# First self attention of a Perceiver block: order of the weight loads, of the masked keys and bias adds, and of the first tile's scores

## The chip, the cores and the metric

The kernel runs on one core of a Trainium2 chip. The metric is the device time in microseconds of one execution, the median of several.

## The reference

The kernel computes one forward pass over x (16 sequences of 64 rows, 256 wide; 1024 rows in all) and a context of 1601 rows for each sequence, in float32. Six layers follow each other, each added to x and each behind a layer norm: cross attention to the context, the self attention with rotary positions that the change touches, a mixture of eight experts, a mean of the context, a second self attention, and a grouped feed forward. The one that matters here:

```python
x = x + _L0_attn_ref(_layernorm(x, axis=-1), L0_attn_w_qkv, L0_attn_w_out, L0_attn_b_out)

def _L0_attn_ref(x, w_qkv, w_out, b_out):      # H = 16 heads of 16
    q, k, v = jnp.split(x @ w_qkv, 3, axis=-1)
    q, k, v = (heads(q), heads(k), heads(v))
    q = q * cos + rotate_half(q) * sin
    k = k * cos + rotate_half(k) * sin
    dots = jnp.einsum('bhid,bhjd->bhij', q, k) * hd ** (-0.5)
    attn = jax.nn.softmax(dots, axis=-1)
    out = jnp.einsum('bhij,bhjd->bhid', attn, v)
    return out.transpose(0, 2, 1, 3).reshape(b, n, H * hd) @ w_out + b_out
```

## The kernel before

The program is one chain of blocks; in a block each engine has its own hand-written order of instructions, tied together by semaphores, and all engines meet at the end of a block. The 1024 rows are T = 8 tiles of 128 rows (two sequences each). The queries and keys of the first six tiles of this attention are projected early, inside the cross attention, and stored in DRAM (early_out, L297); the last two tiles (columns 768 to 1023) and the values of all eight are projected in `self_attention`.

The block ahead of it is `layer_norm` (L735 to L769). Its SP queue issues the loads that it is given: the six weights q, qr, k, kr, v and o (qr and kr are the weights with turned columns, for the rotary term) and the bias row, all seven counted on one semaphore, w_in. PE turns the normalised rows, ACT and DVE copy them to lnT.

In `self_attention` with rope and early (the first use, tag "sa"):

- SP (L910 to L915) waits for the early queries and keys to be in DRAM, loads them to QT and KTt counted on early_in, and then issues the loads of the experts' weights, some 12 MB.
- PE waits for w_in in full (L926), then computes the values in 8 units of 16 matmuls, n = 0 to 7, into two banks in turn (L928). DVE takes the even units out of the banks (L1059), ACT the odd ones (L1179). Both write to Vd, which DVE and POOL have set to zeros and ones before (L893, L894). Then come 8 projection units of 6 matmuls, in the order q, qr for two chunks and k, kr for two chunks (L942), in the same two banks: unit m waits for the taking out of unit m - 2. DVE multiplies a unit with the cosines (L1078), or with the sines (L1082) and adds (L1084). The weights are used as a high part made by ACT (L1187) and a low part made by POOL (L1025).
- After all projections (`projected(pe, 2)`) PE computes the scores of tile 0 (L958), and then runs over the tiles: in step t the scores of tile t + 1, the turning of the output of t - 1 (L986), the transposes of the probabilities (L967), the output projection of t - 1 (L994), the weighing of the values (L977). There is one pair of banks for the scores, SC, so scores t + 1 wait for DVE's subtraction of tile t.
- The scores need masked keys, Km: for each of four head rows a copy of the keys with the other rows zeroed. ACT makes the first (L1141), POOL the other three in two chunks (L1035, six operations for a tile). There are two buffers of them; tiles 0 and 1 are made ahead, tile t + 2 after the scores of tile t.
- POOL: zeros and ones, four weight splits, then the bias adds to X (eight operations, L788, in `add_bias`), then Km of tiles 0 and 1, then `projected(pool, 2)` and the others.
- DVE: after the last projection, per tile the maximum over each head's scores (L1099) and its subtraction (L1101), `less_max`; the normalising (L1108, L1110); and the adding of the output to X (L1116) with its statistics (L1119).
- ACT: values placed to Vt (L1135), keys (L1141), `projected(act, 2)`, then per tile the exponentials (L1148), the copy of the transposes (L1154) and of the turned output (L1160).

The second self attention (tag "sb") calls the same function without early and rope, and its keys need no mask.

## Time and profile before

| | us |
|---|---|
| median of 3 runs | 1307.55 |
| lowest and highest | 1303.25, 1313.32 |
| the profiled execution's time | 1307.01 |
| its span, first to last instruction | 1305.2 |
| PE busy | 1169.1 |
| DVE busy | 690.0 |
| ACT busy | 576.6 |
| POOL busy | 413.7 |

Times in the profile are microseconds from the start of the span unless ns is written. PE is TensorE's matmuls, PEld its weight loads, DVE VectorE, ACT ScalarE, POOL GpSimd, SP the engine that issues the transfers. A row of the timeline gives start, duration, engine, line, operation, output and inputs, shape and count, and in brackets the idle time before it and what ended it. The granted clock (PEclk) is TensorE's: 1.00 is 2.4 GHz, 0.50 is 1.2 GHz.

### The profile page before, as it was taken

To read this page: it belongs to the slowest core of one execution; us is meant where nothing else is said; L and a number is where in the kernel's file an instruction comes from. 1 tells how busy PE (TensorE), PEld (TensorE's weight loads), DVE (VectorE), ACT (ScalarE), POOL (GpSimd) and SP (SyncE) were. 2 spreads that over 40 slices of the span, in tenths; PEclk is the share of its full clock that TensorE was granted. 3 is DMA by queue.
4 is the path that set the end of the run, shared out by engine and by line. 5 is a ranking of instruction groups with operands and counts; after the bars stand their busy time and mean duration, and the time that the engine had idled before them with its cause. 6 is when DMAs were issued, how large, how long until landed. Compare 5 with 4: busy or idle time off the path is not lost. (4 is left out here: it accounts for less than half of the span.)

```text
span 1305.2 us, 32520 instructions
## 1 busy us (share of the span) xinstructions
PE 1169.1 (90%) x13911; PEld 1030.4 (79%) x13911; DVE 690.0 (53%) x1100; ACT 576.6 (44%) x953; POOL 413.7 (32%) x369
## 2 busy tenths in 40 slices
PE   4799999999999999999999999768796999288799
PEld 4789989999999999989999888656674777266588
DVE  6555655655655655655654743347462221564732
ACT  4465555555555555555555565326421232121400
POOL 5632432432432432432432416453351000522000
PEclk9899999999999999999999999979797999588999
DMA  6937646746746746746656743192021111405055
GB/s 200 212 79 170 159 92 159 164 97 163 159 98 161 163 97 157 163 100 160 157 104 147 165 89 78 51 365 107 10 97 52 53 61 53 133 10 213 2 186 190
DMA packets 63143, 165.70 MB, mean 127 GB/s; under 512 B 25032, under 2 KB 38424, under 8 KB 59928
## 3 DMA queue, kind: packets, MB, share of 16 engines
q1 hardware_dynamic: 60312, 158.37, 47.7%
q0 software_dynamic: 1536, 4.20, 0.9%
q8 instruction: 111, 1.82, 0.6%
q10 hardware_dynamic: 1152, 1.05, 0.2%
q14 instruction: 32, 0.26, 0.1%
HBM read 73.18 MB, written 11.01 MB: 65 GB/s over the span
## 5 line engine op out<-in xcount | busy, mean ns | idle before, releaser
L504 DVE TENSOR_REDUCE xa_mx<-xa_sc 128x2 f32<-128x804 f32 x256 | 243.3, 991 | 42.1 <-PE xa_sc L665 42.1
L458 ACT ACTIVATE xa_pt<-xa_sc 128x1024 f32<-128x1024 f32 (+1 forms) x224 | 212.3, 963 | 108.7 <-PE xa_sc L681 108.4
L681 PE MATMUL xa_sc<-xa_queries,xa_keys 104*128 104x128 f32 (+1 forms) x1664 | 221.5, 276 | 0.9 <-issue 0.4
L681 PEld LDWEIGHTS xa_sc<-xa_queries,xa_keys 104*128 104x128 f32 (+1 forms) x1664 | 196.5, 187 | 18.1 <-issue 4.5
L590 PE MATMUL xa_pj<-xa_ctx_hi,xa_wk 128*128 128x400 f32 (+1 forms) x512 | 157.6, 350 | 1.2 <-DVE xa_qst L532 0.9
L590 PE MATMUL xa_pj<-xa_wv,xa_ctx_hi 128*128 128x256 f32 (+1 forms) x832 | 155.2, 285 | 0.1
L692 PE MATMUL xa_op<-xa_pt,xa_values 128*32 128x64 f32 x6656 | 136.3, 222 | 9.0 <-ACT xa_pt L458 4.1
L665 PE MATMUL xa_sc<-xa_keys,xa_queries 96*128 96x402 f32 x512 | 134.5, 364 | 10.8 <-DMA xa_keys<-xa_kst_hi 7.5
L337 POOL TENSOR_TENSOR xa_ctx_lo<-xa_raw,xa_ctx_hi 128x1600 fp32r<-128x1600 f32 (+1 forms) x32 | 115.9, 3624 | 78.0 <-DVE xa_ctx_hi L497 75.3
L342 POOL TENSOR_TENSOR xa_kst_lo<-xa_wk,xa_kst_hi 128x400 fp32r<-128x400 f32 x64 | 67.4, 1053 | 228.4 <-ACT xa_kst_hi L411 228.3
L590 PEld LDWEIGHTS xa_pj<-xa_wv,xa_ctx_hi 128*128 128x128 f32 (+1 forms) x832 | 126.1, 184 | 7.9 <-issue 6.3
L692 PEld LDWEIGHTS xa_op<-xa_pt,xa_values 128*32 128x32 f32 x6656 | 103.5, 109 | 28.0 <-ACT xa_pt L458 15.8
L590 PE MATMUL xa_pj<-xa_wv,xa_ctx_lo 128*128 128x256 f32 (+1 forms) x416 | 116.4, 280 | 0.0
L424 ACT ACTIVATE xa_values<-xa_pj 128x256 f32<-128x256 f32 (+1 forms) x208 | 69.4, 382 | 97.2 <-PE xa_pj L590 97.1
L665 PEld LDWEIGHTS xa_sc<-xa_keys,xa_queries 96*128 96x128 f32 x512 | 90.8, 191 | 23.3 <-DVE xa_mx L504 12.0
L590 PEld LDWEIGHTS xa_pj<-xa_ctx_hi,xa_wk 128*128 128x128 f32 x512 | 97.3, 191 | 2.6 <-DVE xa_qst L532 1.3
L570 DVE COPY xa_o<-xa_op 128x128 f32<-128x128 f32 x32 | 9.3, 292 | 169.7 <-PE xa_op L692 169.7
L590 PE MATMUL xa_pj<-xa_ctx_lo,xa_wk 128*128 128x400 f32 (+1 forms) x256 | 89.2, 348 | 0.0
L342 POOL TENSOR_TENSOR xa_kst_lo<-xa_wv,xa_kst_hi 128x400 fp32r<-128x400 f32 x64 | 67.6, 1056 | 55.2 <-ACT xa_kst_hi L411 55.1
L408 ACT ACTIVATE xa_wk<-xa_pj,xa_bk 128x400 f32<-128x400 f32 x64 | 38.1, 595 | 96.7 <-PE xa_pj L590 96.2
L590 PEld LDWEIGHTS xa_pj<-xa_wv,xa_ctx_lo 128*128 128x128 f32 (+1 forms) x416 | 76.6, 184 | 0.0
L536 DVE RECIPROCAL xa_rec<-xa_pj 128x256 f32<-128x256 f32 x16 | 28.1, 1758 | 78.9 <-PE xa_pj L650 78.9
(322 smaller groups left out, 1779.0 us busy)
## 6 DMA issues: line engine op xcount, KB each, us to landing
xa_keys<-xa_kst_hi SPq DMA_DIRECT2D x256, 200.2 KB, 6.1
xa_keys<-xa_kst_lo SPq DMA_DIRECT2D x128, 200.2 KB, 5.3
xa_raw<-in_ctxT SPq DMA_DIRECT2D x15, 1601.0 KB, 9.3
gf_w<-in_gf_w SPq DMA_DIRECT2D x16, 1024.0 KB, 7.1
moe_ex<-in_moe_ex SPq DMA_DIRECT2D x8, 1088.0 KB, 15.0
xa_queries<-xa_qst SPq DMA_DIRECT2D x96, 32.0 KB, 4.7
moe_slots_in<-in_moe_zero SPq DMA_DIRECT2D x1, 2944.0 KB, 18.1
moe_xs<-moe_slots_in SPq DMA_DIRECT2D x23, 128.0 KB, 2.2
```

The costliest lines, as they stand in the source:

```text
L337: nc.gpsimd.tensor_tensor(ctx_lo[:, :, lo:hi], raw[:, :, lo:hi], ctx_hi[:, :, lo:hi].bitcast(f32), ALU.subtract).then_inc(lo_done, 1)
L342: nc.gpsimd.tensor_tensor(kstage[h][1][:, lo:hi], kraw[u % 2][:, 0:hi - lo], kstage[h][0][:, lo:hi].bitcast(f32), ALU.subtract).then_inc(k ...
L408: nc.scalar.activation(kr[:, 0:hi - lo], PJ[bank(step)][:, 0:hi - lo], ACT.Identity, bias=bk[:, h:h + 1]).then_inc(free["K"], 1)
L424: ins = nc.scalar.activation(vdst[:, kk], vsrc[:, kk], ACT.Copy)
L458: nc.scalar.activation(PT[ptslot(step)][0:rows, 0:nt], SC[bank(step)][0:rows, 0:nt], ACT.Exp, scale=float(D0) ** -0.5).then_inc(ex_done, 1)
L504: nc.vector.tensor_reduce(mx[:, u // 2, 2 * (u % 2):2 * (u % 2) + 2], SC[bank(step)][:, :, 0:MXN], AX.X, ALU.max).then_inc(mx_done, 1)
L536: nc.vector.reciprocal(rec[:], PJ[bank(step)][:, 0:4 * S].rearrange("p (a n) -> p a n", a=4)).then_inc(rec_done, 1)
L570: nc.vector.tensor_copy(o_sb[:, 2 * h:2 * h + 2], OP[h][:, 0:2 * S].rearrange("p (a n) -> p a n", a=2)).then_inc(o_ev, 1)
L590: last = mm(out, l, r, start=n_ == 0, stop=n_ == len(todo) - 1)
L665: last = mm(SC[bank(step)][:, kk, 0:MXN], QS[b % 2][0:96, pr, :], KS[0:96, pr, lo:lo + MXN], start=True, stop=True)
L681: last = mm(SC[bank(step)][0:rows, kk, a * P:(a + 1) * P], KS[:, 2 * a + h, kt * P:kt * P + rows], QS[b % 2][:, 2 * a + h, :], start=True, ...
L692: last = mm(OP[h][32 * j:32 * j + 32, a * S:(a + 1) * S], V[b % 2][0:rows, kt, hd * VW:hd * VW + 32], PT[ptslot(("st", b, h, u))][0:rows, ...
```

## The change

Four things move; no instruction of computation is added or removed.

1. The loads in the layer norm's block are now v, q, qr, k, kr. v has a semaphore of its own (v_landed), and the values' projection waits for it alone; `loaded` counts the four others. The output weight and the bias row are issued in the attention's block, behind the early queries and keys and ahead of the experts' loads, and counted with the early ones on late_in. Who waited for early_in now waits for all four.
2. POOL makes the masked keys of tiles 0 and 1 ahead of the bias adds.
3. PE computes the scores of tile 0 after the four units of q and ahead of the four of k. DVE does `less_max(0)` at the same point, ahead of the taking out of k's units. PE's wait for all projections stands after k, ahead of the second scores.
4. ACT does the exponentials of tile 0 ahead of its wait for all projections.

Without early (the second attention) `ahead_of_scores` is the number of all units, and PE, DVE and POOL keep their order.

```diff
-        loaded = 16 * (len(names) + 3)
+        loaded = 16 * (len(names) if early else len(names) + 3)
...
+            early_from, early_done, v_landed, late_in, late = early
...
+        ahead_of_scores = nproj // 2 if early else nproj
...
         def projected(eng, half):
             per_half = nproj // (2 - own)
             if early:
-                eng.wait_ge(early_in, 16 * 2)
+                eng.wait_ge(late_in, 16 * (2 + len(late)))
...
@@ sync
                 for a, src in zip((QT, KTt), early_from):
-                    sp.dma_start(a[:, :, 0:skipped], src).then_inc(early_in, 16)
+                    sp.dma_start(a[:, :, 0:skipped], src).then_inc(late_in, 16)
+                for dst, src, counted in late:
+                    sp.dma_start(dst, src).then_inc(counted, 16)
@@ tensor
-            pe.wait_ge(w_in, loaded)
+            pe.wait_ge(*((v_landed, 16) if early else (w_in, loaded)))
...
             def before():
+                projections(range(ahead_of_scores))
+                projected(pe, 1 if early else 2)
+                scores(0, 0)
+                projections(range(ahead_of_scores, nproj))
                 projected(pe, 2)
-                scores(0, 0)
@@ gpsimd
-            add_bias(nc, pool, X, bias, w_in, loaded, bias_added)
...
                 projected(pool, 1)
                 for t in range(2):
                     place(t, t)
+            add_bias(nc, pool, X, bias, *((late_in, 16 * (2 + len(late))) if early else (w_in, loaded)), bias_added)
+            if Km:
                 projected(pool, 2)
                 for t in range(2, T):
                     place(t, t % 2)
@@ vector
             for m, (name, ch, g) in enumerate(order):
+                if m == ahead_of_scores:
+                    less_max(0)
...
-            over_tiles(dve, step, lambda: less_max(0), lambda: add(T - 1))
+            over_tiles(dve, step, lambda: less_max(0) if ahead_of_scores == nproj else None, lambda: add(T - 1))
@@ scalar
                     place_keys(t, t)
+                exps(0)
                 projected(act, 2)
-                exps(0)
@@ program
-            row, row_load = bias_row(nc, parts, "sa", a["sa_bo"], w_in)
-            layer_norm(nc, 1, ln, X, stats, lnT, c, loads=loads + row_load)
+            v_landed, late_in = [parts.enter_context(nc.semaphore(n)) for n in ("sa_v_landed", "sa_late_in")]
+            row, row_load = bias_row(nc, parts, "sa", a["sa_bo"], late_in)
+            by_name = dict(zip(W, loads))
+            values_load = [by_name["v"][:2] + (v_landed,)]
+            late = [by_name["o"][:2] + (late_in,)] + row_load
+            layer_norm(nc, 1, ln, X, stats, lnT, c, loads=values_load + [by_name[n] for n in ("q", "qr", "k", "kr")])
```

## Rows read from the trace of the kernel before

**Rows 1.** The page's first part: busy us, share of span, instructions, of TensorE

```profile
PE 1169.1 (90%) x13911; PEld 1030.4 (79%) x13911; DVE 690.0 (53%) x1100; ACT 576.6 (44%) x953; POOL 413.7 (32%) x369
```

**Rows 2.** Waits of 845 to 885 us: total, times, longest

```profile
PE sa_OV L928 <- DMA sa_brow<-in_sa_bo: 5.1, 1, 5.1
```

**Rows 3.** Timeline of SP's queue, 843 to 885 us

```profile
847.08 0.33 SPq L735 DMA_DIRECT2D sa_w_q<-in_sa_q  x1
...
852.54 0.60 SPq L915 DMA_DIRECT2D moe_gate<-in_moe_gate  x1
...
857.87 16.12 SPq L915 DMA_DIRECT2D moe_ex<-in_moe_ex  x6
```

**Rows 4.** Timeline of TensorE, 843 to 885 us

```profile
849.29 1.22 PE L769 MATMUL ln_ps<-consts,ln_y 128*128 128x128 f32 x4 [3.28 <-DVE ln_y L747]
855.57 9.79 PE L928 MATMUL sa_OV<-sa_w_v,lnT 128*64 128x128 f32 x128 [5.06 <-DMA sa_brow<-in_sa_bo]
...
868.49 0.28 PE L942 MATMUL sa_OV<-sa_lnH,sa_wl_qr 128*128 128x256 f32 x1
...
878.00 1.99 PE L958 MATMUL sa_SC<-sa_Km,sa_QT 64*64 64x256 f32 x16 [5.75 <-POOL sa_Km L1035]
882.63 1.98 PE L958 MATMUL sa_SC<-sa_Km,sa_QT 64*64 64x256 f32 x16 [2.64 <-DVE sa_Sc L1101]
```

**Rows 5.** Timeline of POOL, 843 to 885 us

```profile
869.63 6.08 POOL L788 TENSOR_TENSOR X<-X,sa_brow 128x256 f32<-128x256 f32 x8
875.67 4.33 POOL L1035 TENSOR_TENSOR sa_Km<-sa_KT,consts 128x128 f32<-128x128 f32 x12
```

**Rows 6.** Timeline of VectorE, 843 to 885 us

```profile
850.55 0.42 DVE L751 COPY lnT<-ln_ps 128x256 f32<-128x256 f32 x1 [0.99 <-PE ln_ps L769]
...
872.14 0.41 DVE L1078 TENSOR_TENSOR sa_KT<-sa_OV,consts 128x256 f32<-128x256 f32 x1
...
872.91 0.85 DVE L1084 TENSOR_TENSOR sa_KT<-sa_KT,sa_rot 128x256 f32<-128x256 f32 x1
880.04 1.23 DVE L1099 TENSOR_REDUCE sa_mx<-sa_SC 128x16 f32<-128x1024 f32 x1 [6.28 <-PE sa_SC L958]
```

**Rows 7.** Timeline of TensorE, 880 to 926 us

```profile
889.13 1.09 PE L958 MATMUL sa_SC<-sa_Km,sa_QT 64*64 64x256 f32 x16
...
890.43 1.04 PE L967 MATMUL sa_TP<-consts,sa_Pr 128*128 128x128 f32 x8
...
893.73 1.09 PE L958 MATMUL sa_SC<-sa_Km,sa_QT 64*64 64x256 f32 x16
```

**Rows 8.** Transfers of 840 to 900 us: count, KB each, us from issue to landing

```profile
moe_ex<-in_moe_ex SPq DMA_DIRECT2D x6, 1088.0 KB, 17.2
...
sa_KT<-early_k SPq DMA_DIRECT2D x1, 768.0 KB, 8.1
...
sa_w_q<-in_sa_q SPq DMA_DIRECT2D x1, 256.0 KB, 2.6
```

**Rows 9.** Timeline of the second attention's start, VectorE and TensorE

```profile
1161.95 0.69 DVE L751 COPY lnT<-ln_ps 128x512 f32<-128x512 f32 x1 [0.87 <-PE ln_ps L769]
...
1162.96 1.36 PE L928 MATMUL sb_OV<-sb_w_v,lnT 128*64 128x128 f32 x10 [1.05 <-PEq L718]
```

**Rows 10.** Stages: length, busy (instructions) by engine, granted clock, DMA share, GB/s

```profile
845.75:849.00 3.25, 0.26 (x3) 0.07 (x1) 1.48 (x7) 1.49 (x2) 0.00 (x0) 1.00 0.28 68
849.25:859.25 10.00, 4.90 (x38) 4.36 (x40) 4.04 (x7) 0.80 (x2) 2.24 (x2) 0.50 0.95 324
...
876.50:886.50 10.00, 5.44 (x39) 3.24 (x40) 3.84 (x4) 2.74 (x3) 7.47 (x21) 0.50 1.01 424
886.75:927.50 40.75, 31.59 (x458) 24.38 (x456) 28.36 (x56) 26.26 (x37) 8.94 (x25) 1.00 0.06 26
```

**Rows 11.** Timeline of ScalarE, 880 to 960 us

```profile
882.62 1.28 ACT L1148 ACT_TABLE_LOAD   x1 [13.36 <-DVE sa_Sc L1101]
...
926.97 1.36 ACT L1244 ACTIVATE moe_gu<-moe_ex 128x1408 fp32r<-128x1408 f32 x1
```

More of the change, by code:

```diff
@@ L857, in self_attention @@
             columns[1] = (skipped, T * P)
-            early_from, early_done = early
-            early_in = sem("early_in")
+            early_from, early_done, v_landed, late_in, late = early
         turned = ("", "r") if rope else ("",)
@@ L931, in _, with projections, project_unit @@
             pe.wait_ge(ln_lo, CH)
-            for m, (name, ch, g) in enumerate(order):
+            def projections(units):
+                for m in units:
+                    project_unit(m, *order[m])
+            def project_unit(m, name, ch, g):
                 n = T + m
@@ L1065, in _, with less_max @@
                     nc.vector.tensor_tensor(lnL[:, k], lnT[:, k, skipped:], lnH[:, k].bitcast(f32), ALU.subtract).then_inc(ln_lo, 1)
+            def less_max(t):
+                dve.wait_ge(s_full, t + 1)
+                ge(dve, exp_done, t)
+                src = SC[:].rearrange("p e n -> p (e n)")[:, 0:heads * S].rearrange("p (h s) -> p h s", s=S)
+                if conv_bias is not None:
+                    halves = lambda a: a[:].rearrange("p (e h) s -> p e (h s)", e=2)
+                    nc.vector.scalar_tensor_tensor(halves(Sc), SC[:, :, 0:heads * S // 2], float(dk) ** -0.5, halves(CB),
+                                                   ALU.mult, ALU.add).then_inc(bias_done, 1)
+                    dve.wait_ge(bias_done, t + 1)
+                    src = Sc[:]
+                nc.vector.tensor_reduce(mxt[:], src, AX.X, ALU.max).then_inc(mx_done, 1)
+                dve.wait_ge(mx_done, t + 1)
+                nc.vector.tensor_tensor(Sc[:], src, mxt[:].unsqueeze(2).to_broadcast([P, heads, S]), ALU.subtract).then_inc(sub_done, 1)
             turns = 0
             for m, (name, ch, g) in enumerate(order):
+                if m == ahead_of_scores:
+                    less_max(0)
                 n = T + m
@@ L1087, in _ @@
                 dve.wait_ge(cb_in, 16 * 3)
-            def less_max(t):
-                dve.wait_ge(s_full, t + 1)
-                ge(dve, exp_done, t)
-                src = SC[:].rearrange("p e n -> p (e n)")[:, 0:heads * S].rearrange("p (h s) -> p h s", s=S)
-                if conv_bias is not None:
-                    halves = lambda a: a[:].rearrange("p (e h) s -> p e (h s)", e=2)
-                    nc.vector.scalar_tensor_tensor(halves(Sc), SC[:, :, 0:heads * S // 2], float(dk) ** -0.5, halves(CB),
-                                                   ALU.mult, ALU.add).then_inc(bias_done, 1)
-                    dve.wait_ge(bias_done, t + 1)
-                    src = Sc[:]
-                nc.vector.tensor_reduce(mxt[:], src, AX.X, ALU.max).then_inc(mx_done, 1)
-                dve.wait_ge(mx_done, t + 1)
-                nc.vector.tensor_tensor(Sc[:], src, mxt[:].unsqueeze(2).to_broadcast([P, heads, S]), ALU.subtract).then_inc(sub_done, 1)
             def normalise(t):
@@ L1864, in program @@
                                            q=wide, qr=wide, k=wide, kr=wide, v=[P, CH, 2, P], o=[P, 2, D])
-            row, row_load = bias_row(nc, parts, "sa", a["sa_bo"], w_in)
-            layer_norm(nc, 1, ln, X, stats, lnT, c, loads=loads + row_load)
-            self_attention(nc, "sa", att, X, stats, lnT, c, W, w_in, row, H0, D0, D0, c["quarter"], rope=True, loads=expert_loads, early=(early_qk, early_done))
+            v_landed, late_in = [parts.enter_context(nc.semaphore(n)) for n in ("sa_v_landed", "sa_late_in")]
[4 more added lines that the diff above has]
+            layer_norm(nc, 1, ln, X, stats, lnT, c, loads=values_load + [by_name[n] for n in ("q", "qr", "k", "kr")])
+            self_attention(nc, "sa", att, X, stats, lnT, c, W, w_in, row, H0, D0, D0, c["quarter"], rope=True, loads=expert_loads, early=(early_qk, early_done, v_landed, late_in, late))
         y = moe_stack.enter_context(nc.sbuf_tensor("moe_y", [P, T, D], f32))
```

## The prediction, as it stood before the run

> **What bounds the kernel now.** The page's first part comes first: TensorE is busy for 90% of the span [rows 1], and the chain that ended last is TensorE's grouped layers alone, so for a stage in the middle the question is what TensorE waits for there and whether what follows starts with it. The table of stages puts the first self attention (the "sa_" tiles) between 851 and 925 us. Then the waits of 845 to 885 us: two of TensorE's gaps stand out, 5.1 us before the values' projection, released by the last of seven weight transfers, and 5.8 us before the first scores, released by POOL's masked keys [rows 2, 4]. The timelines, engine by engine, give the order.
>
> After the last copy of the normalised rows (to 850.97) TensorE could start, but its first matmul is at 855.57: line 926 waits for all seven transfers, and the last issued, the bias row, lands last [rows 2 to 4]. The values take 9.8 us, and the projection of q ends at 868.77. POOL, when it has split the last weight, at 869.63, adds the bias to X for 6.08 us and only then writes the keys of tiles 0 and 1, 4.33 us for twelve operations; the first scores start at 878.00, right behind [rows 4, 5]. Their maxima and the subtraction, two passes of 1.23 us over one bank pair, take VectorE 2.5 us from 880.04 on, and the second scores start at 882.63 [rows 4, 6]. From there a ring with a period of 4.60 us runs to the end of the attention (scores of tile 2 at 889.13, of tile 3 at 893.73) [rows 7]. So a microsecond won before 889.13 shifts the whole ring, and all behind it that isn't held by something else. This point, the third tile's scores, is where I sum.
>
> **The values' weight first.** It is issued at 847.08 in the place of q, whose transfer landed after 2.6 us [rows 3, 8], so at 849.7: before the rows are normalised. TensorE then starts as in the second attention, where no load is late: 0.32 us after VectorE's last copy (1162.64 to 1162.96) [rows 9]. That is 850.97 + 0.32 = 851.3 in place of 855.57, a gain of 4.3 us. What is late next: VectorE must set zeros and ones before its first eviction, but has done so by 853.9, when the second unit of values still runs; nothing more to pay. The four q and k weights land about 0.5 us later than before, by 853.2, and ScalarE wants the first only after the fourth unit, near 857.9. So values, weight splits and q's projection all move 4.3 us: q ends at 864.5, POOL's last split at 865.4.
>
> **What the moved loads do.** The output weight and the bias row are now issued behind the early queries and keys, in the place of the gate at 852.54 [rows 3], each 0.43 us; the expert loads behind them on SP move by 0.9 us. I put their landing at the 8.1 us of the early keys: 853.0 + 8.1 = 861.1 [rows 8]. The first to wait is ScalarE at about 863, then TensorE at 864.5, POOL at 865.4 (behind ScalarE's wait: the copied values and its keys; behind POOL's: all masked keys and the adds). Cost nothing; the far bound is the experts' 17.2 us [rows 8], landing at 870.2 and 4.8 us lost at POOL.
> The Trainium skill, page "DMA: Bandwidth & Descriptors", section "Queues, rings and completion order", says that each DMA engine takes its ring's descriptors in order, which speaks against this part: two small transfers that waited for little now stand behind 1.5 MB. The landings agree that this is some 8 us and not nothing; by the rule and by the row alike, there is slack.
>
> **Masked keys ahead of the adds.** POOL goes from 865.4 straight to tile 0: six operations of 0.36 us, 2.2 us, done at 867.6. Before, the sixth of the twelve operations was done at 875.67 + 2.17 = 877.84 and the scores started 0.16 us later; so here at 867.75. TensorE has then waited 3.2 us, where it had nothing before. Tile 1's keys end at 869.8, the adds take 6.1 us to 875.9, tile 2's keys are ready at 878.1, a little before they are needed (below). If the adds ran at their slowest beside VectorE (0.91 us each, an estimate from their mean of 0.76, that is 7.3 us) it would be 879.3, still in time.
>
> **Scores and maxima in the middle.** The scores cost TensorE 1.99 us at the low clock (1.2 GHz) [rows 4], 1.09 us at the high one [rows 7]. Which it will be is the open term: after a gap of 3.28 us before the transposes of the layer norm the clock was down (0.50 from 849.25) [rows 4, 10], and before the gap it was at 1.00. A gap of 3.2 us is next to that, so I take the low clock for these scores: 867.75 to 869.75. VectorE takes its 2.5 us, to 872.3. TensorE meanwhile does the first two units of k, whose banks are free (q's four units took 3.3 us, so 0.83 us each at the high clock, twice that at the low one; hidden under VectorE's 2.5 us or nearly), and then waits for VectorE: the third unit needs the first one's bank. VectorE's work on k was beside TensorE; it now comes after the maxima in one piece: two products and an addition per pair, 0.41 + 0.41 + 0.85 = 1.67 us, twice is 3.35 us [rows 6], ending at 875.65. Nothing is removed here: the maxima move from behind k to ahead of it, and k's evictions move by as much. What is gained is that both lie in the time in which POOL used to add. The second scores at 875.75 in place of 882.63: 6.9 us of gain so far.
> ScalarE's table load of 1.28 us [rows 11] and the first exponentials, which stood between maxima and transposes, now end near 874.7, beside k. The old first steps ran at the low clock: 882.63 to 889.13 is 6.5 us. At the high clock the same way takes the ring's 4.6 us, less the turning of a previous output, which stands between scores and transposes (890.22 to 890.43 [rows 7]) and which tile 0 doesn't have; I take 4.4: third scores at 880.15, and 889.13 - 880.15 = 9.0 us gained. The chain needs the clock to have risen again during k; from 876.5 to 886.5 it stayed at 0.50 with TensorE busy 54% [rows 10].
>
> **Sum.** 4.3 (values) + 2.6 (second scores, beyond that) + 2.1 (the first steps at the high clock) = 9.0 us. Behind the attention the experts are next: the last of their loads is issued by 874.0 and lands by some 891, and the first use is at 926.97 [rows 3, 8, 11]; 9 us earlier and 0.9 us later still leave 26 us, so the gain passes. The second attention runs the same order (its keys aren't masked and it has no early load). The profiled execution took 1307.0 us (span 1305.2): 1298.0. The median of before, 1307.55, is 0.5 us over that execution, so I give 1298.5, 0.7% less.
>
> **Bounds.** High clock throughout: scores(0) end at 868.85, everything 0.9 us earlier, gain 9.9, 1297.6. Low clock from the first scores to the first transposes: the last two units of k take 1.66 us each and are not hidden (872.7 to 876.0, with the last product and addition 877.3), and the way from second to third scores is the old 6.5 us less the 0.3 us that they waited for exponentials: 883.5, gain 5.6, 1301.9. What the clock does outside is in the spread: the three runs of before lie 10 us apart.
> The Trainium skill, page "TensorE: Matmul & The Clock Gate", section "What's actually happening", says that the chip's look at the engine's activity runs freely and doesn't start with the kernel, so that the moment of a rise varies from run to run. No single trace can show that. By it, the values, which start at the low clock as before, could stay there up to some microseconds longer than the 3.7 us of this trace; the sum would lose 1 us or so.
>
> **The rivals.**
> (a) The clock doesn't fall in the 3.2 us gap: 1297.6. For: during the 40.75 us from 886.75 with TensorE busy 78% it never fell [rows 10]. Against: the 3.28 us gap.
> (b) The clock falls and doesn't rise before the first transposes: 1301.9. For: the 10 us at 0.50 with as loose a pattern.
> (c) Only the first part pays: the moved loads land as late as the experts' (4.8 us lost at POOL), or k's evictions plus the tile 2 keys hold the third scores as long as the old order did. Gain about 4.3 us, 1303.2. For: DMA is full from 852 on. Against: the loads issued just behind the early keys landed like them.
> (d) Slower: the clock stays low through the attention, since TensorE's work is now in more and shorter pieces. A tile then costs 0.9 us more in the scores (1.99 for 1.09), 0.86 in the transposes (1.04 us [rows 7] by the same ratio) and, an estimate, 0.8 in the output: 2.5 us; seven tiles are 17.5, less the 5.6 of (b): 11.9 slower, 1319.4. It decides from the third tile at the low clock on (5.6 / 2.5 = 2.2). Against: once the ring ran, the clock was high for its length.
> (e) No change beyond noise: TensorE's 3.2 us wait merely moved. Included in (c), since the wait before the values goes in any case.
>
> **How the numbers follow.** Forecast 0.40, (a) 0.33, (b) 0.14, (c) 0.10, (d) 0.03. A measurement of this kernel tells about 1% (13 us) from no change. No case but (d) reaches a loss of 1%, and none by itself a gain of 13 us: forecast and (a) reach it only if the clock elsewhere adds 3 us, for which I give 0.12 out of their 0.73. So faster 0.12, within 1% 0.85, slower 0.03. The range takes in (a), (b) and (c) and the spread of runs: 1293.5 to 1303.5.
>
> **What would show it.** Right: first values matmul near 851.3, released by no DMA; masked keys from 865.4, before the adds; first scores near 867.8 and only two units of k before a wait on VectorE; second scores near 875.8, third near 880.2, ring still 4.6 us. Wrong: a wait of ScalarE or POOL for the bias row's or output weight's transfer; scores of tile 2 released by POOL; clock 0.50 beyond 880.

## The result, and the profile after

| | before | changed |
|---|---|---|
| median, us (13 runs each) | 1308.11 | 1298.82 |
| lowest to highest, us | 1303.25 to 1313.32 | 1295.80 to 1302.85 |
| profiled execution, us | 1307.01 | 1298.63 |
| its span, us | 1305.2 | 1296.8 |

The ratio is 0.9928, with a 95% interval of 0.9916 to 0.9940: 9.3 us less. Forecast were 1298.5 and a gain of 9.0. The two agree almost to the digit, and the trace shows that they agree by luck: the stage that I summed gives 5.5 us, and the rest comes from places that stood in no term of the sum (below).

TensorE through the stage, against [rows 4, 7] (timeline of the changed kernel; start, duration, engine, line, operation, shape and count, idle time before it and what ended it):

```profile
851.12 10.78 PE L930 MATMUL sa_OV<-sa_w_v,lnT 128*64 128x128 f32 x128 [0.78 <-PEq L718]
...
868.64 1.99 PE L964 MATMUL sa_SC<-sa_Km,sa_QT 64*64 64x256 f32 x16 [3.34 <-POOL sa_Km L1042]
870.56 0.58 PE L948 MATMUL sa_OV<-sa_lnH,sa_wh_k 128*128 128x256 f32 x1
...
877.79 1.99 PE L964 MATMUL sa_SC<-sa_Km,sa_QT 64*64 64x256 f32 x16 [2.31 <-DVE sa_rot L1108]
879.71 1.66 PE L973 MATMUL sa_TP<-consts,sa_Pr 128*128 128x128 f32 x8
882.58 1.13 PE L983 MATMUL sa_OV<-sa_Vt,sa_PT 128*64 128x34 f32 x32 [1.21 <-ACT sa_PT L1165]
883.64 1.09 PE L964 MATMUL sa_SC<-sa_Km,sa_QT 64*64 64x256 f32 x16
```

The values start at 851.12, behind no transfer: the 5.06 us wait of [rows 2, 4] is gone. The first scores are at 868.64 in place of 878.00, 9.4 us earlier. But the second are at 877.79 (4.8 earlier than the 882.63 of before) and the third at 883.64 (5.5 earlier than 889.13). So half of what was won by the first scores is lost again before the second. The ring behind them still has a period of 4.60 us.

VectorE, against [rows 6] (timeline of the changed kernel):

```profile
870.68 1.23 DVE L1086 TENSOR_REDUCE sa_mx<-sa_SC 128x16 f32<-128x1024 f32 x1 [4.24 <-PE sa_SC L964]
871.94 1.23 DVE L1088 TENSOR_TENSOR sa_Sc<-sa_SC,sa_mx 128x1024 f32<-128x1024 f32 x1
873.09 0.42 DVE L1104 TENSOR_TENSOR sa_KT<-sa_OV,consts 128x256 f32<-128x256 f32 x1
873.52 0.43 DVE L1108 TENSOR_TENSOR sa_rot<-sa_OV,consts 128x256 f32<-128x256 f32 x1
873.98 2.48 DVE L1110 TENSOR_TENSOR sa_KT<-sa_KT,sa_rot 128x256 f32<-128x256 f32 x1
876.38 0.41 DVE L1104 TENSOR_TENSOR sa_KT<-sa_OV,consts 128x256 f32<-128x256 f32 x1
876.72 0.41 DVE L1108 TENSOR_TENSOR sa_rot<-sa_OV,consts 128x256 f32<-128x256 f32 x1
877.16 0.43 DVE L1110 TENSOR_TENSOR sa_KT<-sa_KT,sa_rot 128x256 f32<-128x256 f32 x1
```

and POOL beside it, against [rows 5] (timeline of the changed kernel):

```profile
866.13 4.51 POOL L1042 TENSOR_TENSOR sa_Km<-sa_KT,consts 128x128 f32<-128x128 f32 x12
870.61 5.57 POOL L788 TENSOR_TENSOR X<-X,sa_brow 128x256 f32<-128x256 f32 x8
```

The two additions on k are the same instruction on tiles of one size. The second takes 0.43 us, the first 2.48: it ends at 876.46, 0.28 us after POOL's last bias add (870.61 + 5.57 = 876.18). Before, the two took 0.96 and 0.85 us beside the same adds [rows 6].

The second scores read the queries and keys of the second tile, which were projected early, so they need nothing of k's work here. They stand behind it because PE's wait for all projections, `projected(pe, 2)`, stands ahead of them. No run moved that wait.

The clock, against [rows 10] (stretches of the changed kernel: length; busy time with instructions of TensorE, its weight loads, VectorE, ScalarE and POOL; granted clock; DMA share and GB/s):

```profile
857.25:867.25 10.00, 8.01 (x99) 7.00 (x95) 5.47 (x12) 7.93 (x15) 6.36 (x7) 1.00 1.01 341
867.50:874.00 6.50, 5.29 (x30) 3.96 (x31) 3.23 (x5) 0.80 (x1) 6.50 (x14) 0.50 1.10 353
874.25:877.25 3.00, 1.23 (x11) 1.03 (x9) 2.96 (x4) 0.01 (x1) 1.93 (x3) 1.00 1.01 359
877.75:880.75 3.00, 2.96 (x21) 1.93 (x22) 0.91 (x1) 0.51 (x1) 2.93 (x9) 0.50 1.00 413
881.00:917.50 36.50, 30.74 (x456) 23.84 (x454) 26.82 (x44) 24.32 (x34) 9.94 (x28) 1.00 0.27 112
```

It rises only at 857, six microseconds into the values, falls at 867.3 in the gap before the first scores, rises at 874.1 in the third of k's four units, and falls a second time at 877.5, in the 2.3 us wait before the second scores. Those and the transposes behind them are then slow.

The early loads (transfers of 840 to 900 us; count, KB each, us from issue to landing), against [rows 8]:

```profile
sa_w_v<-in_sa_v SPq DMA_DIRECT2D x1, 256.0 KB, 2.7
...
sa_w_o<-in_sa_o SPq DMA_DIRECT2D x1, 256.0 KB, 7.2
...
sa_brow<-in_sa_bo SPq DMA_DIRECT2D x1, 128.0 KB, 8.3
```

The bias row, issued at 853.01, is there at 861.3, ahead of anyone who waits for it.

The stage ends 5.4 us earlier than before, and so does the mixture of experts. In the mean of the context the gain becomes 6.5, where the clock rose 9 us earlier (at 1133.6 for 1142.6); no step of the change is in that. In the second attention it becomes 8.2. There the changed kernel has (timelines of ScalarE, then TensorE)

```profile
1181.51 1.28 ACT L1159 ACT_TABLE_LOAD   x1
...
1192.89 0.69 PE L964 MATMUL sb_SC<-sb_KT,sb_QT 64*64 64x64 f32 x32 [0.99 <-DVE sb_Sc L1082]
1194.91 1.11 PE L973 MATMUL sb_TP<-consts,sb_Pr 128*128 128x128 f32 x4 [1.32 <-ACT sb_Pr L1159]
```

and the kernel before

```profile
1200.81 1.28 ACT L1148 ACT_TABLE_LOAD   x1 [12.79 <-DVE sb_Sc L1101]
...
1199.33 0.69 PE L958 MATMUL sb_SC<-sb_KT,sb_QT 64*64 64x64 f32 x32 [0.90 <-DVE sb_Sc L1095]
1202.79 1.11 PE L967 MATMUL sb_TP<-consts,sb_Pr 128*128 128x128 f32 x4 [2.76 <-ACT sb_Pr L1148]
```

The fourth part of the change holds here as well: ScalarE no longer waits for all projections between its last copy and its first exponential, so the load of its function table (ACT_TABLE_LOAD), which stands right ahead of the first exponential, starts 11.4 us before the second scores instead of behind VectorE's subtraction. From second scores to transposes it is 2.02 us in place of 3.46: 1.44 us won.

### The profile page after: what moved, and what is told of

Its sections match the earlier page's. It is cut to its first block and busy times, and to the rows that moved or that the text cites. A ratio compares the mean times of both kernels' runs of the same rounds, so it can differ in the third digit from the quotient of the medians.

```text
span 1296.8 us, 32521 instructions
## 1 busy us (share of the span) xinstructions
PE 1173.1 (90%) x13911; PEld 1034.5 (80%) x13911; DVE 692.1 (53%) x1100; ACT 577.0 (44%) x953; POOL 413.2 (32%) x369
## 5 line engine op out<-in xcount | busy, mean ns | idle before, releaser
L681 PEld LDWEIGHTS xa_sc<-xa_queries,xa_keys 104*128 104x128 f32 (+1 forms) x1664 | 196.5, 187 | 17.9 <-issue 4.3
L665 PEld LDWEIGHTS xa_sc<-xa_keys,xa_queries 96*128 96x128 f32 x512 | 91.1, 191 | 22.6 <-DVE xa_mx L504 11.9
## 6 DMA issues: line engine op xcount, KB each, us to landing
moe_ex<-in_moe_ex SPq DMA_DIRECT2D x8, 1088.0 KB, 15.1
```

The costliest lines, as they stand in the source:

```text
L665: last = mm(SC[bank(step)][:, kk, 0:MXN], QS[b % 2][0:96, pr, :], KS[0:96, pr, lo:lo + MXN], start=True, stop=True)
L681: last = mm(SC[bank(step)][0:rows, kk, a * P:(a + 1) * P], KS[:, 2 * a + h, kt * P:kt * P + rows], QS[b % 2][:, 2 * a + h, :], start=True, ...
```

## The experiments

The theory after the result: the first two parts gain what was forecast or nearly; the third (scores and maxima in the middle) costs time instead of gaining any, since it puts k's work on VectorE, with an addition that POOL's adds hold up, on the path from first to second scores, and opens a second gap for the clock to fall in; the fourth gains in both attentions. The rival: the middle gains as I had written, and the shortfall is the clock's.

Every kernel is compared with runs of the kernel before from the same chip: e1 to e4 and e9 to e12 ran on one chip, e5 to e8 on another. Each experiment has 4 to 6 runs, e9 has 12. Stage times are of one profiled execution each and are told from POOL's first instruction of the stage (851.26 before, 851.08 in the changed kernel), because the stages ahead shift by up to 4 us from one execution to another. "Third" is the start of the third tile's scores, "last" that of the last output projection, both from there.

| kernel | median, us | before, us | ratio (95%) | first / second / third | last |
|---|---|---|---|---|---|
| before | | 1308.11 | | 26.7 / 31.4 / 37.9 | 71.9 |
| changed | 1298.82 | 1308.11 | 0.9928 (0.9916 to 0.9940) | 17.6 / 26.7 / 32.6 | 66.6 |
| changed, again | 1300.64 | 1307.56 | 0.9944 (0.9930 to 0.9958) | 17.5 / 26.6 / 32.4 | 66.5 |
| e1 no middle | 1295.46 | 1307.98 | 0.9906 (0.9892 to 0.9920) | 18.8 / 22.6 / 28.6 | 62.7 |
| e12 the same again | 1295.37 | 1307.56 | 0.9910 (0.9896 to 0.9923) | 17.9 / 21.8 / 28.7 | 63.4 |
| e2 values only | 1303.12 | 1307.98 | 0.9962 (0.9949 to 0.9975) | 23.4 / 28.2 / 35.5 | 71.5 |
| e3 adds early | 1292.84 | 1307.98 | 0.9884 (0.9870 to 0.9899) | 17.5 / 25.4 / 29.8 | 63.9 |
| e4 ScalarE's order undone | 1303.50 | 1307.98 | 0.9963 (0.9949 to 0.9977) | 17.5 / 26.7 / 34.1 | 69.3 |
| e5 spare matmuls | 1285.36 | 1297.66 | 0.9902 (0.9886 to 0.9918) | 16.6 / 25.8 / 31.6 | 66.8 |
| e6 adds early, no middle | 1283.92 | 1297.66 | 0.9895 (0.9880 to 0.9911) | 17.8 / 21.7 / 27.4 | 62.6 |
| e7 ScalarE's order alone | 1292.78 | 1297.66 | 0.9956 (0.9942 to 0.9971) | 26.5 / 31.2 / 37.3 | 71.4 |
| e8 keys first alone | 1291.23 | 1297.66 | 0.9954 (0.9941 to 0.9968) | 22.1 / 25.9 / 33.3 | 68.6 |
| e9 ScalarE's order in the second attention | 1305.83 | 1307.56 | 0.9986 (0.9977 to 0.9994) | 26.6 / 31.2 / 38.7 | 74.6 |
| e10 e6 and spare matmuls | 1290.16 | 1307.56 | 0.9869 (0.9855 to 0.9884) | 16.8 / 20.7 / 25.1 | 59.2 |

Two things have to be kept in mind with this table. First, where the clock rises in the values differs from trace to trace. Of the ten traces with the values first, seven have it 5.6 to 6.0 us in, and the values last 10.7 to 10.8 us; three (e5, e10, e12) have it 2.8 to 3.2 us in, and the values last 9.8:

```profile
853.86 9.82 PE L930 MATMUL sa_OV<-sa_w_v,lnT 128*64 128x128 f32 x128 [0.78 <-PEq L718]
```

It isn't the edits: e12 is e1 once more, and the spare matmuls of e5 and e10 come later. The first scores of the three are about 1 us earlier for it. Second, the medians gain up to 6 us more than the two attentions of the traces account for: e3 gains 15.1 by the medians, and 8.0 (71.9 - 63.9) and 1.4 in the two attentions. So differences of the stage are read from the stage, and the medians say only which way the whole goes.

### The middle taken out (e1, e12)

```diff
-        ahead_of_scores = nproj // 2 if early else nproj
+        ahead_of_scores = nproj
...
-                projected(pe, 1 if early else 2)
+                projected(pe, 2)
                 scores(0, 0)
```

> The change without its third part: scores and maxima of tile 0 behind all projections again, everything else as in the changed kernel. Theory (the middle costs): TensorE has k's four units to do while POOL makes the keys, so there is no gap before the first scores, they run at the high clock near 869.6, the second scores follow the subtraction near 873.3 and the third scores near 878.3, when POOL has the keys of tile 2: 5 us faster than the changed kernel, about 1294. Rival (the prediction's sum): the middle brings the second scores forward, so without it the kernel is not faster than the changed one: 1299 or more.

Measured: 1295.46, 3.4 us under the changed kernel; the third scores at 28.6 for 32.6. TensorE (timeline of e1):

```profile
868.99 1.09 PE L964 MATMUL sa_SC<-sa_Km,sa_QT 64*64 64x256 f32 x16 [1.14 <-POOL sa_Km L1042]
872.88 1.98 PE L964 MATMUL sa_SC<-sa_Km,sa_QT 64*64 64x256 f32 x16 [2.79 <-DVE sa_Sc L1088]
878.88 1.09 PE L964 MATMUL sa_SC<-sa_Km,sa_QT 64*64 64x256 f32 x16
```

With k ahead of the first scores the wait for POOL's masked keys is 1.14 us for 3.34, and the scores run at the high clock. They come 1.2 us later than in the changed kernel, but the second follow 3.9 us behind the first, where they follow 9.2 behind: VectorE has taken out k while POOL made the keys, when VectorE had nothing else to do. In its timeline the additions on k are 0.67 and 0.43 long, beside POOL's keys. The second scores are slow here as well: the clock falls at 872.9, in the 2.79 us wait ahead of them.

The pair was run once more, both at one time on one chip.

> The changed kernel once more, on the same chip as its version without the middle. Both theories: 0.7% faster than before (ratio 0.9928); VectorE's first addition of k again held until POOL's adds end (2.4 to 2.5 us), the clock down in the gap before the first scores.

> e1_no_middle once more, beside e11_changed_again. Theory (the middle costs): 3 us faster than e11_changed_again, the first to the last product of the attention 62.7 us in place of 66.6. Rival (the distance of e1_no_middle was a draw of the clock): within 1 us of e11_changed_again.

Measured: 1300.64 and 1295.37, third scores at 32.4 and 28.7, VectorE's first addition again 2.45 us. So the third part costs 3.4 and 5.3 us in two pairs of medians, and 3.9 and 3.7 at the third scores (3.9 and 3.0 at the last output projection). In the second pair the clock worked both ways: e12's values were 0.9 us shorter than e11's, and it then stood low from 872.0 to 882.3, e11's from 876.7 to 880.1. The rival, that the middle gains, falls.

### One part each (e2, e8, e7, e4, e9)

Only the values' weight first: e1 with POOL's adds back ahead of the keys, and ScalarE's exponentials behind its wait.

```diff
-        ahead_of_scores = nproj // 2 if early else nproj
+        ahead_of_scores = nproj
...
-                projected(pe, 1 if early else 2)
+                projected(pe, 2)
...
+            add_bias(nc, pool, X, bias, *((late_in, 16 * (2 + len(late))) if early else (w_in, loaded)), bias_added)
+
             def place(t, j):
...
-            add_bias(nc, pool, X, bias, *((late_in, 16 * (2 + len(late))) if early else (w_in, loaded)), bias_added)
-            if Km:
                 projected(pool, 2)
...
+                projected(act, 2)
                 exps(0)
-                projected(act, 2)
```

> Only the first part of the change: values' weight first, output weight and bias row behind the early loads; POOL, VectorE, TensorE and ScalarE in their old order. Theory: everything up to the third scores moves by 4.3 us, less up to 1 us if the values stay longer at the low clock: 1304 to 1305. Rival (the wait at the keys absorbs it): POOL is the bound of the first scores and moves with the values anyway, but if the moved loads land late it doesn't: 1307 or more.

Measured: 4.9 us less than before by the medians. In the trace the first scores are 3.3 us earlier, the third 2.4, the last output projection 0.4: the clock was low from 870.3 to 890.8, through the first three tiles, where before it rose at 886.6. This profiled execution was the slowest of its runs, 1308.22, so the medians speak here and the trace shows what the clock can take back. What the part gives in the stage of an ordinary execution no trace shows.

Only the masked keys ahead of the adds, in the kernel before:

```diff
-            add_bias(nc, pool, X, bias, w_in, loaded, bias_added)
...
                 for t in range(2):
                     place(t, t)
+                add_bias(nc, pool, X, bias, w_in, loaded, bias_added)
                 projected(pool, 2)
                 for t in range(2, T):
                     place(t, t % 2)
+            else:
+                add_bias(nc, pool, X, bias, w_in, loaded, bias_added)
```

> The kernel before with only the second part: POOL's masked keys of tiles 0 and 1 ahead of the bias adds, loads and the other engines as before. Theory (POOL's adds were the 5.8 us wait): first scores behind k's last eviction at 873.9 in place of 878.0, without a gap in which the clock falls, third scores 5 to 6 us earlier unless POOL has the keys of tile 2 only at 882.3; that bounds the gain at 889.1 - 882.5 = 6.6: 1302 to 1303. Rival (the prediction's sum put the second scores' 2.6 us to the middle and the keys together): 1305.5.

Measured: 6.4 us less; first scores 4.6 us earlier, the last output projection 3.4; the other 3 us have no place in the trace. TensorE's gap before the first scores is 1.13 us for 5.75.

Only ScalarE's order:

```diff
-                projected(act, 2)
                 exps(0)
+                projected(act, 2)
```

> The kernel before with only the fourth part: ScalarE's first exponentials ahead of its wait for all projections. Theory (the table load leaves the path): 1.4 us in the second attention, from second scores to transposes 2.0 in place of 3.5 us, and 1 to 1.3 us in the first, where the transposes waited for the exponentials until 885.03: 1305.3. Rival (the prediction: the second attention is untouched, the first gains only with the other parts): 1307 or more.

Measured: 4.9 us less. The table load is at 870.79, beside k. The trace has 0.6 us in the first attention and 1.35 in the second (2.11 us from second scores to transposes); for the other 3 it has no place, and what they are is not shown.

The same edit undone in the changed kernel:

> The changed kernel with ScalarE's old order: the wait for all projections ahead of the first exponentials, in both attentions. Theory (the new order took the table load of 1.28 us off the path of the second attention): there the load stands behind the subtraction again and the time from second scores to first transposes goes from 2.0 back to 3.5 us: 1.4 us slower than the changed kernel, 1300.3, perhaps 0.3 more from the first attention. Rival (prediction: the second attention is untouched): 1298.8.

Measured: 4.7 us more than the changed kernel. ScalarE (timeline of e4):

```profile
876.54 1.28 ACT L1159 ACT_TABLE_LOAD   x1 [11.93 <-DVE sa_KT L1110]
```

The load is now behind the last of k, and the clock low until 886.6: the third scores at 34.1 for 32.6, the last output projection at 69.3 for 66.6, and the second attention loses its 1.34 us again (3.36 from second scores to transposes). 2.7 + 1.3 is 4.0 of the 4.7. Of the 2.7, 0.4 is the transposes' later start (2.35 us behind the second scores for 1.92); the rest goes with the low clock, which lasted to 36.6 us into the stage for 29.9. Whether the later load brought that is not shown.

The edit in the second attention alone, in the kernel before:

```diff
-                projected(act, 2)
+                if early:
+                    projected(act, 2)
                 exps(0)
+                if not early:
+                    projected(act, 2)
```

> The kernel before with ScalarE's new order in the second attention alone. Theory (the table load is all that it takes away there): from second scores to transposes 2.1 in place of 3.5 us, 1.4 us faster than before, ratio 0.999. Rival (the fourth part's 4.9 us in e7_act_order_alone come mostly from here): ratio 0.997 or less.

Measured: 1.7 us less over 12 runs, ratio 0.9986 (0.9977 to 0.9994). TensorE (timeline of e9):

```profile
1198.27 0.69 PE L958 MATMUL sb_SC<-sb_KT,sb_QT 64*64 64x64 f32 x32 [0.90 <-DVE sb_Sc L1095]
1200.38 1.11 PE L967 MATMUL sb_TP<-consts,sb_Pr 128*128 128x128 f32 x4 [1.41 <-ACT sb_Pr L1148]
```

2.11 us from the one to the other for 3.46. So the missed term is settled: 1.35 to 1.44 us, and the median agrees (the interval is 0.8 to 3.0 us).

### POOL's adds moved away (e3)

POOL has nothing to do from 853.33 to 859.48, ahead of the weight splits. The bias row is loaded right behind v, on a semaphore of its own, and the adds go there.

```diff
+            if early:
+                add_bias(nc, pool, X, bias, row_in, 16, bias_added)
             for m, name in enumerate(split_order):
...
-            late = [by_name["o"][:2] + (late_in,)] + row_load
-            layer_norm(nc, 1, ln, X, stats, lnT, c, loads=values_load + [by_name[n] for n in ("q", "qr", "k", "kr")])
+            late = [by_name["o"][:2] + (late_in,)]
+            layer_norm(nc, 1, ln, X, stats, lnT, c, loads=values_load + row_load + [by_name[n] for n in ("q", "qr", "k", "kr")])
```

> The changed kernel with the bias row loaded right behind the values' weight and POOL's eight bias adds ahead of its weight splits, where it waited 6 us for ScalarE. Theory (POOL's adds hold VectorE's addition of k, 2.48 us in place of 0.85): that addition takes under 1 us, the second scores come 1.6 us earlier: 1297. Rival (the addition waited for something else, or POOL's adds now slow VectorE's and ScalarE's evictions of the values by as much): 1299, and the addition still over 2 us.

Measured: 1292.84, 6.0 us under the changed kernel and 15.1 under before; the stage has 2.8 of the 6.0. POOL (timeline of e3), VectorE's subtractions beside the adds and its additions on k (the same view), and TensorE's second scores:

```profile
852.15 5.98 POOL L788 TENSOR_TENSOR X<-X,sa_brow 128x256 f32<-128x256 f32 x8
...
864.81 4.50 POOL L1047 TENSOR_TENSOR sa_Km<-sa_KT,consts 128x128 f32<-128x128 f32 x12
```

```profile
853.45 0.43 DVE L1077 TENSOR_TENSOR sa_lnL<-lnT,sa_lnH 128x256 fp32r<-128x256 f32 x1
...
856.43 0.42 DVE L1077 TENSOR_TENSOR sa_lnL<-lnT,sa_lnH 128x256 fp32r<-128x256 f32 x1
...
872.66 0.42 DVE L1113 TENSOR_TENSOR sa_KT<-sa_KT,sa_rot 128x256 f32<-128x256 f32 x1
...
874.62 0.42 DVE L1113 TENSOR_TENSOR sa_KT<-sa_KT,sa_rot 128x256 f32<-128x256 f32 x1
```

```profile
875.25 1.09 PE L964 MATMUL sa_SC<-sa_Km,sa_QT 64*64 64x256 f32 x16 [1.13 <-DVE sa_rot L1111]
```

With POOL's adds gone from beside it, the first addition takes 0.42 us. The wait before the second scores is 1.13 us for 2.31; the clock doesn't fall in it and they take 1.09 us. This is the direct test of both halves of what failed in the middle: hold the addition up, and a gap opens in which the clock falls; let it go, and neither happens. The third scores are 2.8 us earlier. The splits are not late for it (the first at 858.09). Nor do the adds hold anything in their new place: VectorE's two subtractions for the low part of the rows (L1077), with both inputs in SBUF as well, take 0.43 and 0.42 us beside them, and it is POOL's row that takes longer, 5.98 us for 5.57.

### Both taken together (e6), and the gaps filled (e5, e10)

e6 is e3 without the middle; the first scores wait only for the keys.

```diff
-        ahead_of_scores = nproj // 2 if early else nproj
+        ahead_of_scores = nproj
```

> Bias adds early as in e3_adds_early, and scores and maxima of tile 0 behind all projections as in e1_no_middle, but without TensorE's wait for VectorE's last eviction ahead of them. Theory (both costs are separate): first scores at the high clock right behind k, second scores right behind the subtraction, third scores 27.5 us after POOL's first instruction of the stage (e3: 29.8, e1: 28.6): 1290.5 to 1291.5. Rival (e3 had already taken what the middle costs, since with POOL idle VectorE's k work is short): 1292.8.

Measured: third scores at 27.4 for e3's 29.8, the last output projection at 62.6 for 63.9; ratio 0.9895 (0.9880 to 0.9911) against 0.9884 (0.9870 to 0.9899) for e3, on different chips. The stage is shorter and the ratios don't tell the two apart: that the middle costs something even with the adds moved is shown by one trace of each (e6's is the fastest of its four runs) and by no median. TensorE waited 2.79 us for VectorE's subtraction before the second scores, and the clock fell at 873.1 and came back at 880.0.

e5 and e10 add matmuls whose results are not read, to see what the clock's fall costs: e5 is the changed kernel with 24 before the first scores and 14 before the second, e10 is e6 with 20 before the second scores.

```diff
+            def keep_busy(n):
+                for x in range(n):
+                    mm(WP[:, 0, 0:256], WH["q"][:, 0, 0:P], lnH[:, 0, 0:256], start=True, stop=True)
...
+                if early:
+                    keep_busy(20)
                 projected(pe, 2)
```

> The changed kernel with 24 spare matmuls of 256 columns (2.9 us) in TensorE's gap ahead of the first scores and 14 (1.7 us) ahead of the second ones, into a bank that nothing uses yet; their results are not read. Theory (the gaps let the clock fall, as in the changed kernel's trace at 867.3 and 877.5): the clock stays at 1.00, first scores 1.09 us in place of 1.99, second ones 1.09, transposes 1.04 in place of 1.66, third scores some 2.5 us earlier, counted from POOL's first instruction of the stage: 30.0 in place of 32.6; the median 1296.5. Rival (the low clock there is hidden behind VectorE): 1298.8.

Measured: the first two scores at the high clock, 1.09 us each, but the third at the low one (1.98): the clock held to 880.9 and was low from there to 887.8. The first addition on k took longer still (timelines of e5, VectorE, then POOL):

```profile
874.77 3.49 DVE L1118 TENSOR_TENSOR sa_KT<-sa_KT,sa_rot 128x256 f32<-128x256 f32 x1
...
872.40 5.58 POOL L788 TENSOR_TENSOR X<-X,sa_brow 128x256 f32<-128x256 f32 x8
```

It starts 2.4 us after the adds began, where the changed kernel's starts 3.4 us after, and ends again 0.28 us after their end (878.26 and 877.98). The second scores come 0.9 us earlier than in the changed kernel (25.8 for 26.7), and that is the shorter time of the values (9.82 for 10.78) with which POOL's adds moved too; what the high clock gave at the first scores, the held addition took. The last output projection is at 66.8 for 66.6. The ratio, 0.9902, is a little under that of the changed kernel, and the stage doesn't explain it.

> e6_adds_early_no_middle with 20 spare matmuls (2.4 us, results not read) in TensorE's gap ahead of the second scores. Theory (the clock falls because of the gaps around the first scores): second scores, transposes and third scores all at 1.00, third scores 26.0 us after POOL's first instruction of the stage in place of 27.4, the attention 61.2 us long in place of 62.6: ratio 0.988. Rival (as in e5_busy the clock only falls later, in the pieces that follow): attention 62.5 us or more, ratio 0.9895.

Measured: 1290.16 (1289.74 to 1291.11), 17.4 us under before; the lowest ratio of all kernels here, though its interval overlaps that of e3. TensorE, and the clock over the whole stage (timeline, then stretches, of e10):

```profile
868.50 1.10 PE L968 MATMUL sa_SC<-sa_Km,sa_QT 64*64 64x256 f32 x16
872.39 1.10 PE L968 MATMUL sa_SC<-sa_Km,sa_QT 64*64 64x256 f32 x16 [0.21 <-DVE sa_Sc L1097]
876.77 1.09 PE L968 MATMUL sa_SC<-sa_Km,sa_QT 64*64 64x256 f32 x16
```

```profile
855.00:912.50 57.50, 50.23 (x664) 40.30 (x660) 40.23 (x68) 34.89 (x54) 28.07 (x59) 1.00 0.62 237
```

The clock is at 1.00 without a break from the values to the end of the attention, and the way from second to third scores is 4.38 us, the 4.4 that the prediction used for this case. Against e6 (on the other chip), whose clock was low for 6.8 us, the third scores are 2.4 us earlier and the last output projection 3.5. Of both, 1.0 us is the earlier rise in the values (first scores at 16.8 for 17.8), which the spare matmuls, issued later, can't have brought; 1.4 and 2.4 us are left for them.

## Why the prediction was right, step by step

The total was right by luck. The sum was 9.0 us at the third scores, and they came 5.5 earlier: to the second scores 4.8 us were gained for 6.9, and from second to third 0.65 for 2.1. Gains that stood in no term made up for it.

- **Values first: 4.3 us.** The start is right (851.3 forecast, 851.12 measured; TensorE waited for nothing but the block's start). But the values lasted 10.78 us instead of 9.79, since the clock rose 6 us into them and not 3.7. The prediction had named this as a loss of 1 us or so and left it out of the sum. The Trainium skill, page "TensorE: Matmul & The Clock Gate", section "What's actually happening", has it that the moment of a rise is free to vary. The traces agree: with the same start and the same work it lies 5.6 to 6.0 us into the values in seven of them and 2.8 to 3.2 in three, and the values take 10.7 to 10.8 or 9.8 us. So the 1 us is a draw, and one that fell against the changed kernel's profiled execution.
- **The moved loads: nothing.** Right: the bias row landed at 861.3 (861.1 forecast) and nobody waited for it.
- **Masked keys ahead of the adds.** Right in kind: first scores at 868.64 for 867.75, behind a gap of 3.34 us (3.2 forecast), at the low clock (1.99). The 0.9 us are the slower values and some 0.1 more of gap.
- **Scores and maxima in the middle: the step that failed.** "It now comes after the maxima in one piece: two products and an addition per pair, 0.41 + 0.41 + 0.85 = 1.67 us, twice is 3.35 us" took 0.85 from a trace in which the addition ran beside POOL's adds in another order. It took 2.48 once and 0.43 once, and all six instructions ran from 873.09 to 877.59, 4.5 us. So the second scores came at 877.79 and not 875.75. And "what is gained is that both lie in the time in which POOL used to add" is wrong even with the addition let go, as far as one trace of each shows (e3 against e6: 29.8 and 27.4). I compared with the old order, in which VectorE's maxima waited for POOL's adds, and credited the middle with what the second part had already done. The comparison that counts is with parts 1, 2 and 4 alone: there k fills the wait for the keys, on TensorE and on VectorE. By the medians the third part costs 3.4 to 5.3 us, where the prediction had it as a part of the gain.
- **The first steps at the high clock: 2.1 us.** Wrong for the changed kernel: a second gap of 2.3 us let the clock fall again, scores 1.99 and transposes 1.66 us for 1.09 and 1.04 [rows 7], and the way from second to third scores was 5.85 us for 4.4. The size of the term itself is sound: where the clock holds (e10) the way is 4.38, and in e3, too, 4.38 (875.25 to 879.63).
- So the third scores: 883.64 for 880.15. The 3.5 us are 0.9 from the values, 1.15 from the middle and 1.45 from the clock. The gain at that point is 5.5 us; case (b), 5.6 by another way, comes nearest.
- **"The second attention runs the same order" is wrong.** It is the other miss, and a gain: the fourth part is not under `early`, and takes a table load of 1.28 us off the path there. 1.44 us in the trace, 1.7 by e9's median. For the first attention the prediction had counted the load as off the path beside k (it was earlier still, at 865.82, ahead of the maxima); it didn't look for the same wait in the second.
- **The end.** 5.4 us from the first attention, 1.1 in the mean of the context, 1.7 in the second attention (1.44 of it the table load), some 0.2 behind: 8.4 in the profiled pair, 9.3 by the medians. The 1.1 belong to where the clock happened to rise; no run here was made for them.

The rivals: (a) didn't happen, the clock fell in the 3.34 us gap. (b) is near in the stage and not in the total. (c), nothing beyond the first part, is refuted by the total and by e8, though one of its two reasons, k's work holding the scores up, is what cost the middle its gain. (d) didn't happen, the clock was back at 880.9. How much a low clock can cost with no edit in the stage is seen in e9, whose profiled execution had the clock low from 875.5 to 892.5 and its last output projection 2.7 us later than before.

What stays open: why the same addition, beside the same adds of POOL, takes 0.85 to 0.96 us in the old order (before, e2, e7, e9) and is held to the end of them in the new one (changed, e4, e5, e11). In the old order POOL's eight adds take 6.07 us, in the new one 5.57, so in the one each gives way a little and in the other VectorE alone; in e3 and e6 it is POOL alone. Also open are the up to 6 us by which the medians gain more than the traces of the two attentions, some 3 us each in e7 and e8. And the parts don't add up: 4.9 + 6.4 + 4.9 = 16.2 us alone, 12.5 together (e1).

## What to carry to other kernels

When two parts of a change open the same window, price each against the kernel that has the other, not against the kernel before: here the reordering of the projections was credited with time that the reordering on POOL had freed, and cost 3.4 to 5.3 us. Independent work (k's projection and its taking out) belongs in the wait of the engine that would otherwise idle, not behind it. And for every function that is called twice, go through each moved line for the second caller too: a wait that stood between ScalarE's last copy and its first exponential cost 1.4 us there, unseen.

## What the runs showed of the hardware

- A VectorE addition with both inputs in SBUF, 0.42 to 0.43 us alone, was held until POOL's whole row of adds was done, 0.28 us beyond their end, in four traces (2.45, 2.46, 2.48 and 3.49 us). VectorE's passes with an input from PSUM ran beside the same adds at their usual 0.42 and 1.23 us. The Trainium skill, page "SBUF — State Buffer", section "Who interferes with whom", says that a VectorE instruction with two SBUF inputs contends with a GpSimd instruction that reads SBUF, and its section "SBUF: two separate sides" that the one that starts later is blocked for the whole of the other's instruction. The traces agree that it is this kind of instruction that is blocked. By the rule it would wait for one add, 5.57 / 8 = 0.70 us, and take 1.1 at most; it waited for three to five in a row, so the measurement decides: a row of POOL instructions can hold it as one. That it must is not so: beside the same eight adds such an instruction took 0.85 to 0.96 us in the old order, and 0.42 or 0.43 in e3 and e6, where one of POOL's adds took up to 0.97 or 0.98 us instead. What decides between the three is not shown.
- In a gap of TensorE of 2.31 us the clock fell a second time (changed, 877.5); in one of 2.79 us it fell too (e1, 872.9), and in one of 1.13 us not (e3). With 20 spare matmuls in the gap and no other edit it stayed at 1.00 for 57.5 us (e10), where it was low for 6.8 us without them (e6); that is one trace of each, and the ratios are 0.9869 and 0.9895.
- An ACT_TABLE_LOAD took 1.28 us in every trace and cost the path 1.35 to 1.44 us where it stood between the subtraction and the exponentials. The Trainium skill, page "ScalarE: Activation LUTs", section "What ACT_TABLE_LOAD costs", gives the same 1.28 us, with a drain of 1.38 us beside it; of a drain the rows here show nothing: in e4 the exponential starts 0.01 us behind the load, and in the changed kernel the load starts 0.03 us behind the copy ahead of it (865.79 to 865.82).
